# Autocorrelation stage of a decoder: cross products ahead of the last two layer norms, which go to ScalarE; x's spectrum between turned lag weights and their spectrum; weight pieces later

## The reference

```python
qf = fft(q); kf = fft(k)                      # over the 128 positions, per feature
corr = ifft(qf * conj(kf)).real
w, idx = top_k(corr, topk)                    # topk = int(2 * log(128)) = 9, per feature
w = softmax(w)
for i in range(topk):                         # v read at position + lag, held at the last one
    out = out + w[..., i] * take(v, minimum(idx[..., i] + pos, L - 1))
x = layernorm(x + out)                        # q is x, k and v are the context
```

## Time and profile before

| | |
|---|---|
| median of 3 runs | 942.32 us (941.69 to 944.61) |
| profiled execution | 944.06 us, its span 942.2 us |
| TensorE busy | 870.5 us, 92% of the span |
| VectorE, ScalarE, GpSimd busy | 582.5, 396.8, 340.8 us |
| mean granted clock | 0.969 |

### The profile page before, as it was taken

The page is one execution under the profiler, slowest core; times in us unless marked ns, Lnnn a source line. Parts: engine busy times, 40 slices in busy tenths (PEclk is TensorE's granted clock), DMA queues, the critical chain, the costliest instruction groups (busy, mean ns, idle before and its releaser), DMA issues.

```text
span 942.2 us, 21361 instructions
## 1 busy us (share of the span) xinstructions
PE 870.5 (92%) x8680; PEld 695.7 (74%) x8680; DVE 582.5 (62%) x1510; ACT 396.8 (42%) x980; POOL 340.8 (36%) x356
## 2 busy tenths in 40 slices
PE   6999998996998989889999898999999999999995
PEld 5677776663445677667777677888998898889983
DVE  3555664475876466445766543897376747765765
ACT  4254343343564132233444243453454364526532
POOL 1112222377786545555777355870000100010001
PEclk9999999898999999889999899999999999999998
DMA  6400000232230210000000011330000010000001
GB/s 220 154 20 14 21 16 21 65 84 88 87 101 12 82 31 23 5 18 17 26 16 18 18 34 48 89 109 29 23 2 2 1 46 2 1 1 23 2 1 45
DMA packets 21809, 38.09 MB, mean 40 GB/s; under 512 B 3328, under 2 KB 7552, under 8 KB 21456
## 3 DMA queue, kind: packets, MB, share of 16 engines
q1 hardware_dynamic: 21664, 36.66, 12.8%
q10 hardware_dynamic: 48, 0.07, 0.0%
HBM read 30.20 MB, written 2.10 MB: 34 GB/s over the span
## 4 chain that ended last, share of the span: by engine, by line
PE 73%; DVE 10%; POOL 6%; issue 4%; DMA 3%; ACT 2%; SPq 2%; POOLq 0%; DVEq 0%; ACTq 0%
PE bank L745 16%; PE bank L746 15%; PE bank L747 15%; PE bank L866 6%; PE bank L1130 6%; PE bank L887 3%; DVE tank L2288 2%; PE bank L840 2%; PE bank L825 1%; PE bank L871 1%; DVE tank L2298 1%; DVE tank L2078 1%; PE bank L764 1%; SPq L664 1%; PE bank L1150 1%
## 5 line engine op out<-in xcount | busy, mean ns | idle before, releaser
L745 PE MATMUL bank<-wr,hTl 128*128 128x512 f32 (+3 forms) x472 | 192.2, 407 | 5.8 <-DVE wr L2014 2.3
L746 PE MATMUL bank<-wr,hTh 128*128 128x512 f32 (+3 forms) x472 | 182.4, 386 | 0.0
L747 PE MATMUL bank<-wr,hTh 128*128 128x512 f32 (+3 forms) x472 | 182.2, 386 | 0.0
L2078 DVE TENSOR_REDUCE tank<-bank 128x4 f32<-128x512 f32 x128 | 82.4, 686 | 65.9 <-PE bank L840 65.9
L745 PEld LDWEIGHTS bank<-wr,hTl 128*128 128x128 f32 (+1 forms) x472 | 91.1, 193 | 30.6 <-issue 8.8
L1381 ACT ACTIVATE pT<-bank 128x512 f32<-128x512 f32 x128 | 69.5, 595 | 98.7 <-PE bank L840 98.6
L747 PEld LDWEIGHTS bank<-wr,hTh 128*128 128x128 f32 (+1 forms) x472 | 90.6, 192 | 17.9
L746 PEld LDWEIGHTS bank<-wr,hTh 128*128 128x128 f32 (+1 forms) x472 | 91.3, 194 | 15.4 <-issue 1.2
L866 PE MATMUL bank<-qk 32*128 32x128 f32 x1024 | 78.7, 294 | 13.9 <-DVE tank L2078 7.9
L866 PEld LDWEIGHTS bank<-qk 32*128 32x128 f32 x1024 | 66.1, 196 | 30.2 <-issue 20.6
L1353 ACT ACTIVATE qk<-bank,small_sb 128x512 f32<-128x512 f32 x64 | 46.2, 775 | 76.4 <-PE bank L825 76.4
(11 more groups left out here) (234 smaller groups left out, 1918.8 us busy)
## 6 DMA issues: line engine op xcount, KB each, us to landing
raw<-w_qkv_dram SPq DMA_DIRECT2D x12, 256.0 KB, 3.2
raw<-w_xq_dram SPq DMA_DIRECT2D x16, 192.0 KB, 2.4
raw<-w_xo_dram SPq DMA_DIRECT2D x12, 256.0 KB, 2.8
x_all<-x_dram SPq DMA_DIRECT2D x8, 256.0 KB, 6.8
cin<-ctx_dram SPq DMA_DIRECT2D x8, 256.0 KB, 3.5
cin<-ctxT_dram SPq DMA_DIRECT2D x8, 256.0 KB, 3.0
out_dram<-x_all SPq DMA_DIRECT2D x8, 256.0 KB, 2.0
qk<-extra_dram SPq DMA_DIRECT2D x124, 16.0 KB
```

The source lines that it names most:

```text
L745: mm(dst, lhs[1], rhs[0], start=start, stop=False)
L746: mm(dst, lhs[0], rhs[1], start=False, stop=False)
L747: return mm(dst, lhs[0], rhs[0], start=False, stop=stop)
L2078: v.tensor_reduce(nm[b % 2][:, at:at + KT], s_bank[n][:, :].rearrange("p (m t) -> p m t", m=KT), AX, ALU.max, negate=True).then_inc(max_re ...
```

## The change

TensorE: the context's even spectrum of item 3 goes ahead of x's. In period k, x's spectrum of item k + 2 goes between the turning of lag weights k - 1 and their spectrum, and the even spectrum of item k + 2 ahead of correlation k + 1. The transposition of item 0 for the feed-forward step goes into period 6. After the periods, turning 7 goes between the base products of the two items.

ScalarE: the copy of x's spectrum of item 2 goes ahead of the last split of self-attention's output; lag weights 1 are scaled in the ramp, ahead of the copies of item 3; the norms of items 6 and 7 are done here in period 2 (`last_rows`), from a scale and a shift of GpSimd (`last_rstd`).

GpSimd: the norms of items 6 and 7 leave the ramp; their scale and shift are computed in period 2, behind cross products 3. Pieces 3 to 10 are split two periods later (piece k + 1 instead of k + 3), piece 9 right after the periods and piece 10 after the last shift products. The zeroing of rows for item 3 waits for the residual of item 7 and not for its norm.

SyncE: the fetches of pieces 5 to 9 move accordingly: none at items 3 and 4, pieces 5 to 7 at items 5 to 7, the others behind.

```diff
 # SyncE
-                fetch(pieces, 0, 0, PIECES_A0, slice(b + 2, b + 3))
-            fetch(pieces, 0, 0, PIECES_A0, slice(B + 2, B + 4))
+                if b < 3:
+                    fetch(pieces, 0, 0, PIECES_A0, slice(b + 2, b + 3))
+                elif b >= 5:
+                    fetch(pieces, 0, 0, PIECES_A0, slice(b, b + 1))
+            fetch(pieces, 0, 0, PIECES_A0, slice(B, B + 4))
...
 # TensorE, mixture_period(k)
-                if k > 0:
-                    lag_weights_to_lags(k - 1)
-                    lag_spectrum(k - 1)
+                lag_weights_to_lags(k - 1)
+                if k + 2 < B:
+                    x_spectrum(k + 2)
+                elif k == B - 2:
+                    pe.wait_ge(ctxf_ready, 2 * B)
+                    x_to_features(0, 0, MOE, 2)
+                lag_spectrum(k - 1)
+                if k + 2 < B:
+                    even_spectrum(k + 2)
                 if k + 1 < B:
                     correlation(k + 1)
                 if k + 2 < B:
-                    x_spectrum(k + 2)
-                    even_spectrum(k + 2)
                     odd_spectrum(k + 2)
                 if k == B - 1:
-                    pe.wait_ge(ctxf_ready, 2 * B)
                     pe.wait_ge(lagf_ready, 2 * (B - 1))
-                    each(x_to_features, 0, MOE, 2)
+                    x_to_features(0, 1, MOE, 2)
...
 # TensorE, around the periods
             correlation(2)
+            even_spectrum(3)
             x_spectrum(3)
-            even_spectrum(3)
             odd_spectrum(3)
...
-            each(base, 0)
+            base(0, 0)
             lag_weights_to_lags(B - 1)
+            base(0, 1)
             lag_spectrum(B - 1)
...
 # ScalarE
+            def last_rows(b):
+                s = b % 2
+                act.wait_ge(ln_rstd[s], 2)
+                av(x_all[:, b, :], x_all[:, b, :], ACT.Identity, bias=st[s][:, SHIFT], scale=st[s][:, RSTD]).then_inc(x_ready[s], 1)
...
             def mixture_period(k):
-                lag_weights(k - 1)
+                if k > 2:
+                    lag_weights(k - 1)
...
+                if k == 2:
+                    last_rows(B - 2)
+                    last_rows(B - 1)
+                else:
+                    piece_hi(k + 1)
                 if k >= 4:
                     norm_mixture(k - 4)
-                piece_hi(k + 3)
...
             lag_weights(0)
+            x_spectrum(2)
             o_split(0, B - 1)
             lag_weightsT(0)
-            x_spectrum(2)
             for i in range(2):
                 context_spectrum(2, i)
             lag_exp(1)
             lag_spectrum(0)
+            lag_weights(1)
+            context_spectrum(3, 0)
             x_spectrum(3)
-            for i in range(2):
-                context_spectrum(3, i)
-            piece_hi(4)
+            context_spectrum(3, 1)
             for k in range(2, B):
                 mixture_period(k)
+            piece_hi(B + 1)
             each(xT_split, 0, MOE, 2)
             lag_weights(B - 1)
             norm_mixture(B - 4)
             each(gate_exp, 0)
+            piece_hi(B + 2)
...
 # GpSimd
-                    pool.wait_ge(x_ready[1], seq(TRIPS - 1, A0))
+                    pool.wait_ge(branch_added, batch(0, B - 1))
...
+            def last_rstd(b):
+                s = b % 2
+                pool.wait_ge(ln_var[s], seq(b // 2, A0))
+                nc.gpsimd.tensor_tensor(st[s][:, RSTD], st[s][:, MV][:, 1:2], half[:, 0:1], ALU.pow).then_inc(ln_rstd[s], 1)
+                pool.wait_ge(ln_rstd[s], 1)
+                hold()
+                nc.gpsimd.tensor_scalar(st[s][:, SHIFT], st[s][:, MV][:, 0:1], st[s][:, RSTD], -1.0, ALU.mult, ALU.mult
+                                        ).then_inc(ln_rstd[s], 1)
...
             def mixture_period(k):
                 if k + 1 < B:
                     cross_products(k + 1)
                 if k >= 4:
                     rstd_mixture(k - 4)
+                if k == 2:
+                    last_rstd(B - 2)
+                    last_rstd(B - 1)
                 shift_products(k - 1)
-                piece(k + 3)
+                piece(k + 1)
...
             o_rest(0, B - 1)
-            norm_rows(A0, B - 2)
             cross_products(2)
-            piece(3)
             shift_products(0)
-            norm_rows(A0, B - 1)
             rows_without_partner(3)
-            piece(4)
             for k in range(2, B):
                 mixture_period(k)
+            piece(B + 1)
             rstd_mixture(B - 4)
             rstd_mixture(B - 3)
             shift_products(B - 1)
             rstd_mixture(B - 2)
+            piece(B + 2)
```

More of the change, by code:

```diff
@@ L458, in normed @@
             per_trip = {MOE: 2, XA: 1}[y]
-            return nth(trip, per_trip, j, {MOE: 0, XA: 2}[y] * TRIPS)
+            return nth(trip, per_trip, j, {MOE: 0, XA: 2}[y] * TRIPS + 2)
         def one_of(trip):
```

## The result

The changed kernel took 937.06 us in the median of 8 runs (934.61 to 939.89); beside it the kernel before took 942.24 in 8 runs (941.69 to 944.61). The ratio is 0.9939, with a 95% interval of 0.9916 to 0.9962. So the change makes the kernel faster, by about 5.2 us (5.7 by the ratio) in place of the 10.8 summed. 937.06 lies inside the range, 5.6 above the number predicted, and within 1.3 of rival B's 938.3. All ratios here leave out slow executions, of which there was one: 1214.47 us at a mean clock of 0.65, in the experiment with idle matmuls, whose median is 935.06 without it.

What follows compares the result with a forecast made beforehand. TensorE and the loop of even spectrum, copy, swap, products and correlation were both taken as tight; stage -10.45, base -0.8 and pieces +0.5 make -10.8, so 931.5 us median (933.3 profiled), range 928.5 to 939.5.

Steps and rivals of the forecast that it cites:

- rival B: VectorE becomes the bound: masked sums fall among GpSimd's products, three periods give back 2.0 each; 938.3 us, chance 0.24.
- Ramp: Before turning 1: cross products of item 3 start at 226.95, not 233.58; turning 1 at 224.15, not 231.63.
- the half clock: TensorE's half clock level (1.2 GHz) after ramp idle; left open, full clock assumed, would cost 1.2 to 1.6 us.
- Periods 2 to 5: Autocorrelation periods ending with turnings 2 to 5 at 235.6, 246.9, 257.0, 268.4; period 4 TensorE's own work, 10.1 us.
- Sums of items 4 to 6 in the short statistics: VectorE's masked sums fall into GpSimd's short statistics after the cross products, unblocked as at 258.67, 0.29 us each.
- Period 6 at 11.7: Autocorrelation period to turning 6 at 280.1 (before 290.55), with two shifted sums and one moved transposition (0.5): 11.7 us.
- Period 7 at 9.6: Last period keeps 9.6 us, set by copy, lag spectrum, copy, shift products; first expert matmul at 289.7, not 300.15.
- Base, -0.8: Turning 7 before half of the base matmuls: they fill the copy wait, lag spectrum and all behind gain 0.8 us.
- pieces, +0.5: Piece 10 split after the last shift products, fetch of piece 12 waits: between nothing and 1.27, taken as 0.5 us.
- C: SyncE's in-order fetches hold the swaps if splits come 7 us later; nothing is left, 941 to 944 us, chance 0.05.
- D: TensorE granted the half clock for whole periods; slower, 949.5 us with two such periods, chance 0.05.
- the rule that spoke against the change: A vector instruction with two SBUF inputs contends with GpSimd reading SBUF, later blocks fully; applied to every period: 938.3 us.

Runs made afterwards that it cites:

- VectorE's list short: Changed kernel with TensorE's periods in the old order, masked sums reading PSUM, VectorE's copy and last four replacements left out: 935.84 us, ratio 0.9922.
- the best version: Changed kernel with masked sums reading PSUM, VectorE's copy and last four replacements left out: 929.52 us (ratio 0.9849), run again 931.28 us (0.9879).

## Why the prediction was right in its range and off by 5.6 us

All positions of the kernel after are given here with the 3.07 added by which its stage began earlier.

- *Ramp: right.* Correlation 2 at 218.11 (predicted 218.15), idle before it 2.33 (2.6). GpSimd's cross products of item 3 start at 227.19 (226.95). The masked sums of item 1 were blocked (0.69, 1.33, 1.35, 1.34), as reckoned. The clock of the ramp, left open, did fall in this profile: a context spectrum took 1.92 in place of 1.02 (at 217.40 of the trace's own time); turning 1 stands at 225.2, predicted 224.15. That is a little less than the 1.2 to 1.6 priced for the half clock. In the profile with the base products put back, whose ramp is the same and kept full clock, turning 1 comes 14.63 after turning 0, predicted 14.52.
- *Periods 2 to 5: right.* Turnings at 235.97, 247.30, 257.33, 268.67; predicted 235.6, 246.9, 257.0, 268.4. The steady period of 10.03 (predicted 10.1) is the value of TensorE's new order: with the old one and all else changed it is 11.15, and 11.35 with VectorE's list short.
- *Sums of items 4 to 6 in the short statistics: the step that failed.* Item 4's did. Those of items 5 and 6 started 0.13 and 0.59 us behind the first shift product and were blocked; add_mixture behind them started at 262.76 and 275.72 (the trace's own times). The shifted sum of item 5, which stands in period 6 in both kernels, waits for the latter (the mixture of item 3), since it writes the bank that item 3's sum had.
- *Period 6 at 11.7: it took 16.07.* 2.30 is the wait for VectorE and 1.7 the clock in this execution (14.39 where it didn't fall). With the sums from PSUM it was 11.81 with no other step touched. *Period 7 at 9.6: it took 10.60*, 1.0 of it the clock again: where the clock held behind the same wait, as with the sums from PSUM, it took 9.55, so the step itself was right.
- *Missing from the sum: what VectorE's small copies can cost.* I priced its top lags at 5.35 for the item, from a row of before in which both were held up a little, 0.58 and 0.63 in place of 0.17:

```profile
254.25 0.58 DVE L2184 TENSOR_SCALAR stats<-stats 128x4 f32<-128x4 f32 x1
...
256.83 0.63 DVE L2192 COPY lag<-stats 128x4 f32<-128x4 f32 x1
```

In the kernel after the copy alone took 2.91 in item 5, L2215 2.14 in item 6, and the top lags 7.33 and 6.45. From 250.17 to 264.40 VectorE's list took 14.2 us, then 12.9, where rival B reckoned 12.1 and TensorE needs 10.1.
- *Base, -0.8, and pieces, +0.5:* from the first expert matmul to the last lag spectrum's copy the profile after is 0.95 shorter, so the interleaving does what the sum says in that place; with the base products put back it is 0.96 longer again. By the runs neither can be told from nothing.
- *Rival B: this is what happened*, with the mechanism as given (1 us of drift puts the sums among products); I had held it at 0.24. That its price is nearly met, 938.3 against 937.06, is partly luck. B reckoned 2.0 in each of three periods; here VectorE's list ran over in two, by more, and TensorE felt it at one place only, where it had no slack left and where the clock then fell. In the profile 2.30 of the loss is the wait, and most of the rest is the clock, which B didn't price. C and D did not come: no swap waits behind a fetch, no period ran at the half level; each fall of the clock cost 0.9 to 1.7.

On the rule that spoke against the change. A masked sum of the kernel after took 1.29 to 1.35 beside products and 0.29 beside the statistics; with one operand from PSUM, 0.35 beside products. The Trainium skill, SBUF — State Buffer, section Who interferes with whom, gives both halves: a VectorE instruction with two SBUF inputs contends with GpSimd's reads, one with at most one SBUF input does not, outside the modes that use both ports. The trace agrees wherever a sum and a product of 128x512 met in the rows shown. Beside GpSimd's statistics (128x1), which read SBUF too, the sums at 246.70 took 0.29 and were not held up; what part of such a short instruction holds the ports, no run here shows. The same section names copy and tensor_scalar among those that can enter the two-port modes. I read only the half on two inputs; the copy of 2.91 and the tensor_scalar of 2.14 fit the other half. That they use both ports is not shown by a run here, only that they end with GpSimd's products.

What stays open: the worth of the pieces and of the interleaved base, and why the clock fell after 2.3 us of idle in one execution and not in another. The ramp's part of the gain was never undone by itself; with TensorE's periods in the old order 0.9927 is left for it, the pieces and the base together, and that most of this is the ramp is read from the traces. L2215 is still held up in the best version (866 and 712 ns in the mean over 7 in its two profiles, 0.17 us when free); taking it off VectorE wasn't tried.

## What to carry to other kernels

Before two engines are packed tighter, write out the whole list of the third for one new period, with every instruction at its price beside a busy neighbour, not at its price in the old trace; 71 of 96 us busy looked like slack, and in two periods the list was then 3 to 4 us too long. Where a sum comes out right only if a short instruction falls into a gap of 1 us, work out how late it may come, and what stands ahead of it. A gain that is given back by the next engine doesn't show when its own edit is undone (0.9927 against 0.9939): undo it once more with the suspected taker relieved (0.9922 against 0.9849 and 0.9879). And compare the parts of the profiles in which the clock held: here one repeated within 0.02 us, where the stage differed by 3.4.

## What the runs showed of the hardware

- A VectorE copy of 128x4 took 2.91 us, through the end of one GpSimd instruction and two whole products of 1.26 that started behind it; free it takes 0.17. The instruction held up was not let in between the two products. With the sums from PSUM one took 3.06 in the same way.
- A masked sum of 128x128 with accumulation takes 0.29 us with both operands in SBUF and GpSimd quiet, 1.34 beside products, and 0.35 with one operand in PSUM, beside products or not (at most 0.353 in 32 of them). Where it can't be kept out of products, the slower source is the faster one.
- After 2.30 and 2.31 us of idle the same shifted sum took 5.40 in one execution and 3.70 in another, of kernels that differ only behind it.
- The shifted sum of item 6, after 1.16 to 1.22 us of idle and two waits of 0.68 before that, took 5.37 in six of ten profiles; in the other four it kept full clock, and the period was 1.0 us shorter. So idle time of this size has to be priced as a range.
